# Logits by slots: TensorE transposes of a copied tile in place of a second product

## The reference, cut to what matters

```python
xn = rms_norm(x, gamma_x)
se = rms_norm(slot_embeds, gamma_slot)
logits = jnp.einsum('bsd,etd->bset', xn, se)
dispatch = jax.nn.softmax(logits, axis=1)
slots = jnp.einsum('bsd,bset->betd', xn, dispatch)
h = jax.nn.gelu(slots @ w1, approximate=False)
processed = h @ w2
combine = jax.nn.softmax(logits.reshape(b, s, e * t), axis=-1)
out = jnp.einsum('bnd,bsn->bsd', processed.reshape(b, e * t, d), combine)
```

## Time and profile before

| | us |
|---|---|
| median of 3 runs | 525.79 |
| lowest, highest | 525.74, 526.81 |
| the profiled execution | 526.66 |
| its span, first to last instruction | 524.9 |
| TensorE busy | 473.5 |
| VectorE busy | 354.4 |
| ScalarE busy | 319.9 |
| GpSimd busy | 175.4 |

### The profile page before, as it was taken

The page is one execution under the profiler, slowest core; times in us unless marked ns, Lnnn a source line. Parts: engine busy times, 40 slices in busy tenths (PEclk is TensorE's granted clock), DMA queues, the critical chain, the costliest instruction groups (busy, mean ns, idle before and its releaser), DMA issues.

```text
span 524.9 us, 15159 instructions
## 1 busy us (share of the span) xinstructions
PE 473.5 (90%) x5384; PEld 378.6 (72%) x5384; DVE 354.4 (68%) x905; ACT 319.9 (61%) x560; POOL 175.4 (33%) x278
## 2 busy tenths in 40 slices
PE   4049899999999999999999999999999999999996
PEld 2037686877878787787878687787768778787775
DVE  3667587585958768594966858595775859585561
ACT  3225747667573757658484766758476675847562
POOL 4314243251424334152424325141432514243220
PEclk9999999999999999999999999999999999999999
DMA  2220202020020202002020200102020110202000
GB/s 68 64 51 2 51 12 52 1 43 22 12 51 10 50 0 55 5 10 50 10 50 5 55 0 20 40 10 50 10 50 0 37 23 10 41 12 42 12 2 10
DMA packets 45362, 14.41 MB, mean 27 GB/s; under 512 B 35224, under 2 KB 45208, under 8 KB 45336
## 3 DMA queue, kind: packets, MB, share of 16 engines
q1 hardware_dynamic: 44904, 13.80, 12.6%
q10 hardware_dynamic: 432, 0.26, 0.2%
HBM read 3.57 MB, written 2.10 MB: 11 GB/s over the span
## 4 chain that ended last, share of the span: by engine, by line
PE 69%; DMA 14%; ACT 5%; POOL 4%; issue 4%; SPq 2%; DVE 1%; POOLq 0%; ACTq 0%; DVEq 0%
PE x L867 18%; DMA stack_t<-stack 13%; PE p_sa L903 12%; PE x L1016 11%; PE p_ctx L920 8%; PE x L1026 5%; PE p_feat L892 5%; POOL stack L421 3%; ACT stack L478 3%; PE x L945 2%; PE x L933 2%; PE x L972 2%; PE x L980 1%; PE p_sb L903 1%; ACT ctx_sb L495 1%
## 5 line engine op out<-in xcount | busy, mean ns | idle before, releaser
L427 POOL TENSOR_TENSOR s_sb<-s_sb,causal 128x256 f32<-128x256 f32 x128 | 93.5, 730 | 270.5 <-ACT s_sb L490 268.7
L677 DVE TENSOR_SCALAR arg<-p_feat,f_low,f_high 128x512 f32<-128x512 f32 x128 | 103.1, 806 | 29.8 <-PE p_feat L892 27.4
L683 DVE TENSOR_TENSOR s_sb<-p_sa,causal 128x384 f32<-128x384 f32 x128 | 70.3, 549 | 59.7 <-PE p_sa L903 59.6
L490 ACT ACTIVATE s_sb<-p_sb 128x384 f32<-128x384 f32 x128 | 62.5, 489 | 76.7 <-PE p_sb L903 76.3
L903 PE MATMUL p_sa<-feat 64*64 64x256 f32 (+3 forms) x1024 | 100.0, 312 | 7.1 <-ACT s_sb L490 3.7
L485 ACT ACTIVATE feat<-arg,f_bias 128x512 f32<-128x512 f32 x128 | 91.6, 716 | 21.1 <-DVE arg L677 21.1
L903 PEld LDWEIGHTS p_sa<-feat 64*64 64x64 f32 x1024 | 76.2, 134 | 34.6 <-issue 27.5
L903 PE MATMUL p_sb<-feat 64*64 64x256 f32 (+3 forms) x1024 | 100.0, 313 | 0.0
L903 PEld LDWEIGHTS p_sb<-feat 64*64 64x64 f32 x1024 | 76.9, 134 | 0.0
L892 PE MATMUL p_feat<-stack_t,omega_st 96*128 96x256 f16 x256 | 50.8, 280 | 23.4 <-DMA stack_t<-stack 23.0
L1016 PE MATMUL x<-w_sb,hid_t 128*128 128x128 f32 x512 | 59.8, 275 | 0.0
(11 more groups left out here) (134 smaller groups left out, 849.7 us busy)
## 6 DMA issues: line engine op xcount, KB each, us to landing
xin<-in_L_attn_x_dram SPq DMA_DIRECT2D x32, 64.0 KB, 2.4
out_dram<-out_sb SPq DMA_DIRECT2D x32, 64.0 KB, 2.1
se_rows<-n_L_ffn_slot_embeds_dram SPq DMA_DIRECT2D x1, 256.0 KB, 5.9
w_f<-in_L_ffn_w_dram SPq DMA_DIRECT2D x1, 256.0 KB, 6.1
w_sb<-in_L_ffn_w_dram SPq DMA_DIRECT2D x1, 256.0 KB, 4.8
stack_t<-stack SPq DMA_TRANSPOSE x16, 4.3
bqkv_bc<-in_L_attn_bqkv_dram ACTq DMA_DIRECT2D x1, 192.0 KB, 5.1
wqkv_f<-in_L_attn_Wqkv_dram SPq DMA_DIRECT2D x1, 192.0 KB, 5.1
```

The source lines that it names most:

```text
L427: pool.tensor_tensor(v, v, m, ALU.mult).then_inc(mb_ok, 1)
L490: nc.scalar.activation(s_sb[:, p % 4, 1, :], p_sb[:, 0:384], ACT.Copy).then_inc(eb_ok, 1)
L677: nc.vector.tensor_scalar(arg[:, p % 2, :], p_feat[:, :], f_low[:, 0:1], f_high[:, 0:1], ALU.max, ALU.min).then_inc(cl_ok, 1)
L683: nc.vector.tensor_tensor(s_sb[:, p % 4, 0, :], p_sa[:, 0:384], causal[:, :], ALU.mult).then_inc(ea_ok, 1)
```

## The change

The second product is gone. VectorE's `token_maxima` no longer reduces x01 in one instruction. It runs one `tensor_scalar` for each 128 tokens that multiplies by 1 and takes the maximum with -3.0e38, writes that copy to a new tile `log_sb` in SBUF, and gives the maximum over the slots as its accumulated output. TensorE transposes each 128 x 128 block of the copy into x23: 8 transposes for 12 products. `logits` is split: `logits_tokens` stands ahead of `project(b, 4)`, and `logits_turned` behind it.

Two semaphores are new. `lc_ok` is raised by each copy, and TensorE's transposes wait for it. `lt_ok` is raised when a half of x23 is written, and `slot_maxima` waits for it where it waited for `lg_ok`.

```diff
             def token_maxima(b):
 
-                after(dve, lg_ok, count(b, 3, 1))
-                nc.vector.tensor_reduce(maxima[:, 4:6], x01[:, :, :], AX_X, ALU.max)
+                after(dve, lt_ok, count(b, 2, 0))
+                for j in range(TILES):
+                    after(dve, lg_ok, count(b, 2, j + 1))
+                    nc.vector.tensor_scalar(log_sb[:, j, :], x01[:, j, :], 1.0, LOWEST, ALU.mult, ALU.max,
+                                            accum_out=maxima[:, 4 + j:5 + j]).then_inc(lc_ok, 1)
 
             def slot_maxima(b):
 
                 for h in range(2):
-                    after(dve, lg_ok, count(b, 3, 2 + h))
+                    after(dve, lt_ok, count(b, 2, h + 1))
...
-            def logits(b, nxt):
+            def logits_tokens(b, nxt):
                 if nxt:
                     after(pe, qkvs_ok, count(b, 1, 2))
                 after(pe, ge_ok, count(b, 2, 0))
                 hi, lo = xt_hi[:, b[1], :], xt_lo[:, b[1], :]
                 for j in range(TILES):
                     sl = slice(128 * j, 128 * j + 128)
-                    mm = three(x01[:, j, :], hi[:, sl], lo[:, sl], se_hi[:, :], se_lo[:, :], True, False)
-                mm.then_inc(lg_ok, 1)
-                for c in range(NCH):
-                    if c % 2 == 0:
-                        after(pe, (o1_ok, o2_ok)[c // 2], count(b, 1, 0))
-                    sl = slice(128 * c, 128 * c + 128)
-                    mm = three(x23[:, c // 2, T * (c % 2):T * (c % 2) + T], se_hi[:, sl], se_lo[:, sl], hi, lo,
-                               c % 2 == 0, False)
-                    if c % 2 == 1:
-                        mm.then_inc(lg_ok, 1)
+                    three(x01[:, j, :], hi[:, sl], lo[:, sl], se_hi[:, :], se_lo[:, :], True, False).then_inc(lg_ok, 1)
+
+            def logits_turned(b):
+                for j in range(TILES):
+                    after(pe, lc_ok, count(b, 2, j + 1))
+                    for c in range(NCH):
+                        if c % 2 == 0 and j == 0:
+                            after(pe, (o1_ok, o2_ok)[c // 2], count(b, 1, 0))
+                        o = T * (c % 2) + 128 * j
+                        mm = nc.tensor.matmul(x23[:, c // 2, o:o + 128], log_sb[:, j, 128 * c:128 * c + 128],
+                                              ident[:, :], start=(j == 0 and c % 2 == 0), stop=False,
+                                              is_transpose=True, skip_group_check=True)
+                        if j == 1 and c % 2 == 1:
+                            mm.then_inc(lt_ok, 1)
...
+                        logits_tokens(b, nxt)
                         project(b, 4)
-                        logits(b, nxt)
+                        logits_turned(b)
```

More of the change, by code:

```diff
@@ L28 @@
 CLIP = 20.0
+LOWEST = -3.0e38
 BLOCKS = ((0, 0, 0, T, 0), (64, 64, 64, T, 64), (128, 0, 128, 192, 256), (192, 64, 128, T, 256))
@@ L158, in build @@
         maxima = sb("maxima", [128, 6], BF16)
+        log_sb = sb("log_sb", [128, TILES, SLOTS])
         disp = sb("disp", [128, TILES, SLOTS])
@@ L249, in build @@
         lg_ok = sem("lg_ok")
+        lc_ok = sem("lc_ok")
+        lt_ok = sem("lt_ok")
         mx_ok = sem("mx_ok")
```

## The result

| | us |
|---|---|
| before, median of 4 runs | 525.84 (525.74 to 526.81) |
| changed, median of 4 runs | 533.83 (533.32 to 534.41) |
| ratio | 1.0148, 95% interval 1.013 to 1.0166 |
| profiled executions, before and changed | 526.66 and 533.76 |
| their spans | 524.9 and 532.0 |

The changed kernel is slower by 8.0 us. The prediction was 538.2, in a range of 533.0 to 544.5, with 12.4 us as its sum. The direction, the place and the mechanism were right, and the forecast loss was too large by half.

The account below looks back on a forecast made before the run. TensorE is busy 473.5 of 524.9 us, but VectorE was taken to be late at the change. A clip delay of 0.87 us in 14 rows (12.2), plus 0.2 in the first, made 12.4 us: 538.2, range 533 to 544.5.

Parts of the forecast that it names:

- That a wait takes the place of the saving: TensorE at the transposes: 0.43 us a row saved, but it waits there from 226.8 to about 227.8 instead.
- The transposes, the round trip, the slot maxima: Second copy to slot maxima: pickup 0.05 us, transposes of 0.125 + 0.287, pickup 0.05; the maxima then hold VectorE 1.20.
- the rival of the dear ones: New transposes on TensorE run as slowly as the f32 product: four take 1.00 us, 17 us lost, 543; chance 0.03.
- The copies: VectorE's two copies with maxima, in place of one reduction: 1.50 us together, bounds 1.29 and 1.94.
- VectorE is late here, not TensorE: At the token maxima: logits by tokens lie ready, VectorE has no idle time between `qk_norms` (226.95) and the maxima (227.02).
- Both paths are late, so the row is: At the next batch's projection: TensorE's path and the path through `clip(b, 4)` and the stack are both 0.87 us late.
- the DMA's short wait: TensorE's wait for the transposed stack, 0.36 us a row, read as two paths of nearly one length.
- The signs in the profile: Expected after: TensorE idle about 1 us before transposes, first copy to clip 3.2 us, TensorE busy some 7 us less.
- The absorbed case: Stack's path does not move with the clip, so TensorE saves its 0.36 us projection wait: 7 us, about 533; chance 0.08.
- The clock: TensorE slows behind the new wait, from 228.34 to 231.06: +1.5 us a row, 21 us more, 559; chance 0.03.

Follow-up runs that it names:

- e2: Changed kernel with the product by slots put back in place of the transposes, copies and their maxima kept: 526.14 us, ratio 1.0009 to the kernel before.
- e3: Changed kernel with the eight transposes reading a constant tile, so without waiting for the copies, and logits by slots left out: 526.59 us, 30.05 us a row.
- e1: Kernel before with only project(b, 4) moved between the product by tokens and the product by slots: 525.52 us, ratio 0.9994.

## Why the prediction was right, and where its size came from

**That a wait takes the place of the saving: right.** TensorE waits for the copy (0.60 us a row), VectorE waits for the transposes (0.53), and nothing gives it back. e2 takes the transposes out of the round trip and e3 the wait for the copies, and each removed the loss. They show the cause; before them it was argued.

**The transposes, the round trip, the slot maxima: right to a hundredth.** Grouped by shape, the new transposes and the copies read

```profile
L972 PE MATMUL x<-ident,log_sb 128*128 128x128 f32 x128 | 20.3, 286 | 8.9 <-DVE log_sb L716 8.9
```

```profile
L716 DVE TENSOR_SCALAR_CACHE_REDUCE log_sb<-x 128x512 f32<-128x512 f32 x32 | 20.6, 679 | 0.4 <-PE x L874 0.4
```

The transposes have the 0.286 us of the cheap form, one instruction each (128 in 16 rows), so the rival of the dear ones is out. From the end of the second accumulator read, 230.67, to the slot maxima, 231.19, it took 0.52 us (sum: 0.51). The maxima held VectorE for 1.21 (sum: 1.20).

**The copies: the term that was sized too large.** I took 1.50 us for both, with bounds of 1.29 and 1.94. They took 230.67 - 229.37 = 1.30. The rule of the Trainium skill that I had cited (VectorE: DVE Perf Modes, section "Two Vector instructions with no wait between them") is right as far as it goes: each copy comes with a DVE_READ_ACCUMULATOR of its own. But the read lasts 0.08 us, and the first starts at 229.97 together with the second copy, so it holds nothing up. And a copy held the engine for 0.60, as the reductions did. My lower bound, made of the nearest rows alone, was the value. This is 0.20 us a row, 2.8 us of the 12.4.

**"VectorE is late here, not TensorE": wrong, by 0.14 us.** The prediction read the 0.07 us between 226.95 and 227.02 as no idle time and said that the logits by tokens lay ready. They did not. An instruction of VectorE that waits for nobody starts 0.08 before the one ahead of it ends, as `clip(b, 4)` did at 229.36 where the slot maxima ended at 229.44. The token maxima started 0.07 after it, because the last product by tokens ended at 226.59 + 0.39 = 226.98. In the changed kernel the products stand 0.2 us earlier and are taken one tile at a time, and the first copy starts at 229.37, 0.07 ahead of the end of `qk_norms`. So 0.14 us came back in each row, 2.0 us in 14.

The two terms are the difference: 0.87 - 0.20 - 0.14 + 0.02 = 0.55 us, as measured on VectorE. A row got 0.52 us longer. On TensorE the same two terms make `scores(b, 3)` 0.48 us late in a steady row, 4.15 us behind `attention_out` instead of 3.67, where the prediction had 0.73.

**"Both paths are late, so the row is": right, and for a better reason than given.** I had worked out VectorE's side as the longer. In the kernel before it was the shorter or equal: e1 gave it 0.15 us and gained nothing, and e3 took 0.53 from TensorE's and gained 0.06. The prediction used the DMA's short wait as the sign of two paths of one length. There was a second such pair, ahead of `scores(b, 4)`, which I did not look for.

**The signs in the profile.** The wait ahead of the transposes was 0.60 us (forecast: about 1), and from the first copy to `clip(b, 4)` it took 232.40 - 229.37 = 3.03 us (forecast: 3.2). One sign missed by more: TensorE's busy time was to fall by some 7 us and fell by 2.9. The busy time counts a matmul's whole duration, of which the next one covers a good part only where it doesn't wait. In e3, with the same number of matmuls and no wait for the copies, it is 467.2 us, 6.3 less than before.

**The rivals.** The absorbed case (533) was near the measured time by its number, but not by its mechanism. The DMA's wait is unchanged, and the time was lower for the two reasons above. The clock showed no drop behind the new wait: it is in the top tenth in all slices behind the fourth. The prediction had put the slow shape of the earlier trace rows behind the long wait at the start. Of its four slow instructions in the kernel before only two, at 39.2 and 40.2 us, stand behind that wait, which ended at 31.4, and two stand ahead of it, at 11.6 and 12.6.

## What to carry to other kernels

A saving on the busiest engine that sends its input through another engine is worth what that engine's queue lets through. Count the trip both ways, and cover both waits: a cover on one side alone brought 0 and 0.07 us of the 0.52 here, and on both sides the transposes were worth 0.41 us a row against products in the same order, of which that order itself took 0.28. When an engine is 90% busy, look for its short waits before taking work away: two lines moved on an engine that is 61% busy gave 0.9%, and the change with its new order and the same two lines gave 0.7%. And a wait that ends while the instruction before is still under way is not in the waits view: compare start with start.

## What the hardware showed that I had not expected

**An accumulator read cost nothing where a copy followed it.** It was 0.08 us long and started in the same hundredth as the next instruction (229.97 in the rows above).

**A TENSOR_SCALAR with constants took as long as a reduction.** It took 0.68 us for 128x512 out of PSUM, where the clip, the same size with two operands for each partition, took 0.80.

**The clock at the start.** The windows of the changed kernel's start (stretch, its length, busy us and count for five engines, clock, DMA share, GB/s) show TensorE at half clock, that is at 1.2 GHz, and then at full:

```profile
13.00:26.60 13.60, 0.00 (x0) 0.00 (x0) 7.49 (x19) 3.39 (x15) 4.81 (x5) 0.50 0.26 60
26.60:39.90 13.30, 6.97 (x48) 4.89 (x49) 8.68 (x25) 3.98 (x9) 1.82 (x6) 0.50 0.25 50
...
53.20:66.00 12.80, 11.19 (x125) 8.76 (x118) 6.14 (x15) 9.78 (x16) 2.64 (x4) 1.00 0.28 52
```

It had no instruction in the first of these stretches, and worked for 6.97 of 13.30 us at the lower level in the second. The trace of the kernel before gives a full clock in every slice, yet its matmuls there are as slow: up to 522 ns against a median of 337, and the two of this shape at 39.2 and 40.2 us take 522 ns in both traces. The first `attention_out` starts at nearly the same time in both, 73.31 and 73.23. So the clock record of before's start is not to be trusted, and the durations are. A new wait of 0.60 us in every row did not bring the lower level back: the 128 transposes behind it last between 0.27 and 0.33 us throughout.
